# A two-layer graph network in one kernel: shared reads for the prepared sums of the second layer's weights, their low parts on GpSimd, the wait for stores taken off the sync queue, and stage 2 written out on TensorE

## The chip, the cores and the metric

One core of one Trainium2 chip. The metric is device time in microseconds of one execution. Engines: PE is TensorE, DVE is VectorE, ACT is ScalarE, POOL is GpSimd, SP is SyncE, which here does nothing but issue all DMAs of the kernel.

## The reference

```python
h = jnp.maximum(_layernorm(x, axis=-1), 0.0)          # x: 1250 x 1024
def _sage_sum(h, src, dst, Ws, Wn, b):                # Ws, Wn: 1024 x 1024
    h_neigh = jax.ops.segment_sum(h[src], dst, num_segments=N_NODES)
    return h @ Ws + h_neigh @ Wn + b
h = _sage_sum(h, src, dst, Ws1, Wn1, b1)
h = _sage_sum(h, src, dst, Ws2, Wn2, b2)
return x + h
```

There are 41,250 edges, sorted by `dst`, among 1250 nodes. All arrays are 32-bit floats.

## The kernel before, in words

The sum over neighbours is a product with a matrix A of edge counts, 1250 x 1250, so a layer is h Ws + A (h Wn) + b. Each factor is kept as a high part (rounded to the fast matmul type) and a low part (what is left), and a product is three matmuls: high by high, high by low, low by high (`PRODUCTS`). ScalarE makes a high part by a copy, another engine the low part by a subtraction.

Stage 1, to about 174 us, normalizes and transposes h into `HT`, computes y1 = h Wn1 and writes it to DRAM, and builds A in `AT`.

Stage 2 makes the first layer's output h1, transposed, in eight feature tiles of 128 columns (`feature_tile`, line 1138). A tile is two halves on TensorE. The first is 72 matmuls of `HT` with a column block of Ws1, `W_st` (lines 1146), the second 60 matmuls of `AT` with a column block of y1, `y_st` (line 1154). Both blocks have one buffer each, so block j + 1 of W_st is loaded when the first half of tile j is done (semaphore `wst_used`), and that of y_st when its second half is done (`h1_done`). ScalarE makes the high parts (lines 714, 750), VectorE the low parts (lines 966 to 974), ScalarE also writes h1 out of PSUM (`h1_save`, line 756). TensorE ran the tiles in a loop of four rounds of two.

Stage 3 computes h1 Ws2 and h1 Wn2, each by Strassen's seven products of halves: `SEQUENCE` names the 14 products, `LEFT` and `RIGHT` the blocks that are added or subtracted for each, `TARGETS` where it goes. Each product is four steps of 15 matmuls (line 1183). After it the `neighbours` products with A, and the result goes out.

In ten of the 14 products the right factor is a sum of two weight blocks, four steps each: 40 sums of 128 x 512 values. They depend on weights alone and are made during stage 2, beside the feature tiles, and parked in DRAM (`sums_dram`); stage 3 loads one at each step into `right`. A sum takes these steps, with five slots (`PREP`): SP loads both blocks into `prep_raw`, 256 KB each (line 484); GpSimd adds or subtracts them (line 635); ScalarE makes the high part (line 763); VectorE makes the low part (line 961); SP stores both parts, 512 KB (line 497).

The order of that work is written out by hand. Each engine takes its instructions strictly in the order given, and SP has all loads and stores in one such order. Per tile SP issues the load of W_st, four `prepare` steps, the load of y_st, and three `prepare` steps (`PER_TILE`, line 102), until the 40 are done in tile 6. A `prepare(i)` waits until the slot's earlier store has landed, loads the two blocks of sum i, waits for the low part of sum i - 4, and stores it. ScalarE's order in tile j is: high part of W_st j + 1, high parts of three sums, high part of y_st j + 1, h1 of tile j, high parts of four sums. When all sums are stored, SP loads the first three right factors, then b2 and a half of x, which VectorE adds together (line 984) ahead of its work for product 1.

Of the kernel before, what the change touches and what calls it, by code (L numbers as in the profile page):

```python
# [65 lines left out]
PER_TILE = (3, 4)  # L66
# [30 lines left out]
def sum_steps():  # L97

    return [n for n in range(STEPS) if right_is_sum(n // KB)]


def prepared(j, part):

    first = j * sum(PER_TILE) + part * PER_TILE[0]
    return range(first, min(first + PER_TILE[part], len(sum_steps())))

# [123 lines left out]
def gnn_kernel(nc, x, src, dst, ws1, wn1, b1, ws2, wn2, b2, out):  # L230
    edge_rows = nc.dram_tensor("edge_rows", (EROWS + P + 3, ROWX), F16, kind="Internal").ap()
    y1_dram = nc.dram_tensor("y1_dram", (N, D), F32, kind="Internal").ap()
    sums_dram = nc.dram_tensor("sums_dram", (len(sum_steps()), P, 2, HALF), F32, kind="Internal").ap()

    ctx = ExitStack()
    with ctx:
# [68 lines left out]
        prep_raw = at("prep_raw", [P, PREP, 2, HALF], F32, W0)  # L305
# [55 lines left out]
        prep_in = [sem(f"prep_in_{i}") for i in range(PREP)]; prep_stored = [sem(f"prep_stored_{i}") for i in range(PREP)]  # L361
# [33 lines left out]
        def _(sp):  # L395
# [85 lines left out]
            def quarter(n, which, to):  # L481
                what, m = SEQUENCE[n // KB]
                row, col = RIGHT[m][which]
                return sp.dma_start(to, (ws2 if what == "s" else wn2)[row * HALF + n % KB * P:row * HALF + (n % KB + 1) * P,  # L484
                                                                      col * HALF:(col + 1) * HALF])
# [12 lines left out]

            for j in range(KF):
                if j:  # L500
                    sp.wait_ge(wst_used, j)
                    load_w_st(j)
                    for i in prepared(j - 1, 1):
                        prepare(i)
# [8 lines left out]
                for i in prepared(j, 0):  # L513
                    prepare(i)
                if j == KF - 2:
                    for i in range(PREP - 1):
                        prepare(len(sum_steps()) + i)

            def load_right(n):
# [5 lines left out]
                if right_is_sum(n // KB):  # L525
                    sp.dma_start(right[:, KB - 1 - n % KB, :, :].bitcast(F32), sums_dram[right_sums(n), :, :, :]).then_inc(right_in[n % KB], 16)
                else:
                    quarter(n, 0, right_sum[:, KB - 1 - n % KB, LO, :]).then_inc(right_in[n % KB], 16)
# [6 lines left out]
            for i in range(PREP):  # L535
                sp.wait_ge(prep_stored[i], 16 * (len(sum_steps()) // PREP))
# [23 lines left out]
        def _(pool):  # L560
# [100 lines left out]
        def _(act):  # L661
# [99 lines left out]
            def prepare_high(i):  # L761
                act.wait_ge(prep_summed, i + 1)
                nc.scalar.activation(prep[:, i % PREP, HI, :], prep_raw[:, i % PREP, LO, :], ACT.Copy).then_inc(prep_hi, 1)
# [468 lines left out]
```

## Time and profile before

| | |
|---|---|
| median of 3 runs | 743.38 us (743.15 to 746.88) |
| the profiled execution's own time | 745.81 us |
| its span, first to last instruction | 744.0 us |
| TensorE, matmul busy | 663.2 us (89%) |
| VectorE, ScalarE, GpSimd busy | 307.9, 171.8, 160.8 us |
| mean granted TensorE clock | 0.949 |
| DMA | 103.1 MB, mean 139 GB/s |

Busy time is a share of the whole span and stages differ, so it says little by itself. What bounds a stage is read from the waits and from the timeline of that stage. In the rows further down L12 is line 12 of the kernel, SPq is the queue of DMA issues, PEld is TensorE's loading of weights, and "[x <-y]" behind a row is how long the engine stood idle ahead of it and what ended that. In some names the number at the end is left out.

### The profile page before, as it was taken

How to read it: one execution, taken by the hardware profiler on the slowest of the kernel's cores; microseconds unless marked ns; L12 is line 12 of the kernel's file. 1: busy time of each engine (PE TensorE's matmuls, PEld its weight loads, DVE VectorE, ACT ScalarE, POOL GpSimd, SP SyncE). 2: the span in 40 equal slices, each digit the busy share in tenths (PEclk: the TensorE clock that was granted, in tenths of full speed). 3: DMA queues.
4: the chain of work that ended last, by engine and by line, in shares of the span. 5: the costliest groups of instructions: out<-in, count | busy, mean ns of one | idle time of the engine just before them, and what ended most of it. 6: DMA issues, size and time to landing. Idle time of an engine off the chain costs nothing.

```text
span 744.0 us, 8540 instructions
## 1 busy us (share of the span) xinstructions
PE 663.2 (89%) x3280; PEld 571.7 (77%) x3280; DVE 307.9 (41%) x426; ACT 171.8 (23%) x292; POOL 160.8 (22%) x161
## 2 busy tenths in 40 slices
PE   3899999999987676786857999999999999999998
PEld 2688688878977576786757998888887778888786
DVE  3644897731322220222222225613446779731111
ACT  5443422221121210112121221221222433400000
POOL 4514340001412222222213002560311402100000
PEclk9999999999999788787879999999999999999999
DMA  8422410014456666565657456844442224111111
GB/s 297 154 49 49 123 47 32 30 56 147 171 184 220 202 210 219 171 224 182 218 188 246 143 157 216 296 150 158 154 141 73 70 84 143 56 57 57 53 57 55
DMA packets 69630, 103.10 MB, mean 139 GB/s; under 512 B 17313, under 2 KB 35755, under 8 KB 69590
## 3 DMA queue, kind: packets, MB, share of 16 engines
q1 hardware_dynamic: 69590, 102.58, 41.9%
q8 instruction: 24, 0.39, 0.2%
q14 instruction: 16, 0.13, 0.1%
HBM read 71.07 MB, written 31.48 MB: 138 GB/s over the span
## 4 chain that ended last, share of the span: by engine, by line
PE 40%; DMA 21%; issue 20%; POOL 7%; DVE 6%; SPq 4%; ACT 2%; DVEq 0%; POOLq 0%
PE PS L1058 14%; PE PS L1199 12%; DMA sums_dram<-prep 10%; PE PS L1183 6%; DMA W_st_raw<-ws_in 4%; POOL left_sum L655 4%; DMA y_st_raw<-y_dram 4%; PE PS L1050 3%; PE PS L1146 3%; SPq L484 2%; DVE prep L961 2%; POOL s L645 2%; DMA xin<-x_in 1%; DVE W_st L966 1%; DVE y_st L972 1%
## 5 line engine op out<-in xcount | busy, mean ns | idle before, releaser
L1183 PE MATMUL PS<-right,left 128*128 128x512 f32 x840 | 192.7, 390 | 2.6 <-DVE s L1002 2.1
L1183 PEld LDWEIGHTS PS<-right,left 128*128 128x128 f32 x840 | 157.0, 188 | 38.0 <-issue 5.8
L1146 PE MATMUL PS<-HT,W_st 128*128 128x416 f32 (+1 forms) x576 | 120.1, 372 | 21.8 <-DVE W_st L966 20.4
L1146 PEld LDWEIGHTS PS<-HT,W_st 128*128 128x128 f32 x576 | 115.9, 203 | 25.8 <-DVE W_st L966 22.1
L1154 PE MATMUL PS<-AT,y_st 128*128 128x416 f32 (+2 forms) x480 | 103.7, 381 | 35.9 <-DVE y_st L974 35.9
L1154 PEld LDWEIGHTS PS<-AT,y_st 128*128 128x128 f32 (+1 forms) x480 | 99.7, 209 | 39.5 <-DVE y_st L974 37.7
L1058 PE MATMUL PS<-W,HT 128*128 128x512 f32 (+1 forms) x480 | 123.3, 406 | 4.2 <-issue 2.4
L635 POOL TENSOR_TENSOR prep_raw<-prep_raw 128x512 f32<-128x512 f32 x40 | 59.7, 1494 | 239.4 <-DMA prep_raw<-ws_in 153.6
L1058 PEld LDWEIGHTS PS<-W,HT 128*128 128x128 f32 (+1 forms) x480 | 87.2, 189 | 24.4 <-issue 2.8
L655 POOL TENSOR_TENSOR left_sum<-h1T 128x640 f32<-128x640 f32 x24 | 42.5, 1773 | 173.1 <-PE PS L1183 123.7
L1199 PE MATMUL PS<-y_high,AT 128*128 128x512 f32 (+1 forms) x200 | 78.3, 392 | 0.0
L1199 PE MATMUL PS<-y_low,AT 128*128 128x512 f32 (+1 forms) x200 | 78.3, 392 | 0.0
L972 DVE TENSOR_TENSOR y_st<-y_st_raw,y_st 128x1152 fp32r<-128x1152 f32 x8 | 11.9, 1488 | 119.8 <-ACT y_st L751 119.8
L966 DVE TENSOR_TENSOR W_st<-W_st_raw,W_st 128x1024 fp32r<-128x1024 f32 x8 | 9.8, 1226 | 89.6 <-ACT W_st L714 89.6
L1199 PEld LDWEIGHTS PS<-y_low,AT 128*128 128x128 f32 (+1 forms) x200 | 37.1, 186 | 8.9
L1199 PEld LDWEIGHTS PS<-y_high,AT 128*128 128x128 f32 (+1 forms) x200 | 37.0, 185 | 8.7
L1038 DVE TENSOR_TENSOR s<-s,PS 128x512 f32<-128x512 f32 (+1 forms) x20 | 13.8, 688 | 72.1 <-PE PS L1199 72.1
L906 DVE TENSOR_TENSOR hot_n<-iota_n,pair_key 128x1600 f16<-128x1600 f16 x40 | 39.3, 983 | 0.0
L750 ACT ACTIVATE y_st<-y_st_raw 128x1152 fp32r<-128x1152 f32 x8 | 9.3, 1165 | 124.6 <-DMA y_st_raw<-y_dram 124.6
L904 DVE TENSOR_TENSOR hot_m<-iota_m,pair_m 128x1280 f16<-128x1280 f16 x40 | 33.0, 824 | 9.9 <-PE PS L1050 9.8
L1002 DVE TENSOR_TENSOR s<-s,PS 128x512 f32<-128x512 f32 (+1 forms) x60 | 36.4, 679 | 0.0
L1050 PEld LDWEIGHTS PS<-hot_n,hot_m 128*128 128x128 f16 x400 | 27.9, 97 | 8.6 <-issue 6.7
(79 smaller groups left out, 467.0 us busy)
## 6 DMA issues: line engine op xcount, KB each, us to landing
sums_dram<-prep SPq DMA_DIRECT2D x40, 512.0 KB, 4.4
right<-sums_dram SPq DMA_DIRECT2D x40, 512.0 KB, 3.4
prep_raw<-ws_in SPq DMA_DIRECT2D x40, 256.0 KB, 3.4
prep_raw<-wn_in SPq DMA_DIRECT2D x40, 256.0 KB, 3.1
y_dram<-y_out SPq DMA_DIRECT2D x18, 256.0 KB, 2.0
y_st_raw<-y_dram SPq DMA_DIRECT2D x8, 576.0 KB
s<-x_in SPq DMA_DIRECT2D x18, 256.0 KB
out<-s SPq DMA_DIRECT2D x18, 256.0 KB
```

The costliest lines, as they stand in the source:

```text
L635: nc.gpsimd.tensor_tensor(prep_raw[:, i % PREP, LO, :], prep_raw[:, i % PREP, LO, :], prep_raw[:, i % PREP, HI, :], RIGHT[SEQUENCE[n // KB ...
L655: nc.gpsimd.tensor_tensor(left_sum[:, k, LO, :], h1_block(*a, k), h1_block(*b, k), op).then_inc(left_summed, 1)
L904: nc.vector.tensor_tensor(hot_m[:, u % HOT, :, :, :], iota_m[:, :, :].unsqueeze(1).to_broadcast([P, ROW, P, 2]), pair_m[:, u, :, :].unsque ...
L906: nc.vector.tensor_tensor(hot_n[:, u % HOT, :, :, :], iota_n[:, :, :].unsqueeze(1).to_broadcast([P, ROW, NCOL, 2]), pair_key[:, u, :, :].u ...
L972: nc.vector.tensor_tensor(y_st[:, LO, 0:NT - 1, :], y_st_raw[:, LO, 0:NT - 1, :], y_st[:, HI, 0:NT - 1, :].bitcast(F32), ALU.subtract).the ...
L1002: nc.vector.tensor_tensor(c, c, PS[:r, BANKS2[g % 8], :], op).then_inc(dve_evicted, 1)
L1050: ins = nc.tensor.matmul(PS[:, COUNT_BANKS[g % 2], col:col + NCOL], hot_m[:, u % HOT, i, :, e], hot_n[:, u % HOT, i, :, e], start=i == 0, ...
L1058: ins = nc.tensor.matmul(PS[:r, bank, :], HT[:, a, k, t * P:t * P + r], W[:, k, b, :], start=first and m == 0, stop=last and m == 2)
L1146: ins = nc.tensor.matmul(PS[:, banks[c], 0:w_], W_st[:, a, k, :], HT[:, b, k, o_:o_ + w_], start=k == 0 and m == 0, stop=False)
L1154: ins = nc.tensor.matmul(PS[:, banks[c], 0:w_], y_st[:r, part, s, :].bitcast(dt), AT[:r, s, o_:o_ + w_].bitcast(dt), start=False, stop=s = ...
L1183: ins = nc.tensor.matmul(PS[:, BANKS2[g % 8], :], left[:, k, a, i * P:(i + 1) * P], right[:, KB - 1 - k, b, :], start=k == 0 and j == 0, s ...
L1199: ins = nc.tensor.matmul(PS[:rows_of(t), BANKS2[g % 8], :], AT[:r, s, t * P:t * P + rows_of(t)].bitcast(dt), y.bitcast(dt), start=s == 0 a ...
```

## The change

Four things. (1) For a chunk k of 128 rows of Ws2 or Wn2, the five sums of Strassen's scheme use only the four blocks at that chunk. These are now loaded once into a buffer `quarters`, and all five sums are made of them: eight batches of five. (2) The low parts of the sums move from VectorE to GpSimd, two sums behind. (3) SP no longer waits for a slot's store to land; GpSimd does, ahead of the sum that reuses the slot. SP waits for the low part ahead of each store, as it did. The 40 sums are spread over 14 parts, two per tile, up to tile 7. (4) TensorE's loop over the tiles is written out.

```diff
-            def prepare(i):
-
-                if i < len(sum_steps()):
-                    if i >= PREP:
-                        sp.wait_ge(prep_stored[i % PREP], 16 * (i // PREP))
-                    for which in range(2):
-                        quarter(sum_steps()[i], which, prep_raw[:, i % PREP, 1 - which, :]).then_inc(prep_in[i % PREP], 16)
-                if i >= PREP - 1:
-                    e = i - (PREP - 1)
-                    sp.wait_ge(prep_lo, e + 1)
-                    sp.dma_start(sums_dram[e, :, :, :], prep[:, e % PREP, :, :].bitcast(F32)).then_inc(prep_stored[e % PREP], 16)
+            def load_quarters(batch):
+
+                what, k = BATCHES[batch]
+                sp.wait_ge(prep_summed, batch * len(SUMS))
+                for q, (row, col) in enumerate(QUARTERS):
+                    quarter(what, row, col, k, quarters[:, q, :]).then_inc(quarter_in[q], 16)
+
+            def store_sums(part):
+                for i in prepared(part):
+                    sp.wait_ge(prep_lo, i + 1)
+                    sp.dma_start(sums_dram[i, :, :, :], prep[:, i % PREP, :, :].bitcast(F32)).then_inc(prep_stored[i % PREP], 16)
+                    batch, q = divmod(i, len(SUMS))
+                    if q == LOAD_AT and batch + 1 < len(BATCHES):
+                        load_quarters(batch + 1)
...
                     sp.wait_ge(wst_used, j)
                     load_w_st(j)
-                    for i in prepared(j - 1, 1):
-                        prepare(i)
+                    store_sums(2 * j - 1)
...
-                for i in prepared(j, 0):
-                    prepare(i)
-                if j == KF - 2:
-                    for i in range(PREP - 1):
-                        prepare(len(sum_steps()) + i)
+                if j:
+                    store_sums(2 * j)
+                else:
+                    load_quarters(0)
...
-            for i, n in enumerate(sum_steps()):
-                pool.wait_ge(prep_in[i % PREP], 32 * (i // PREP + 1))
-                nc.gpsimd.tensor_tensor(prep_raw[:, i % PREP, LO, :], prep_raw[:, i % PREP, LO, :], prep_raw[:, i % PREP, HI, :],
-                                        RIGHT[SEQUENCE[n // KB][1]][2]).then_inc(prep_summed, 1)
+            def prepare_sum(i):
+                batch, (a, b, op) = i // len(SUMS), RIGHT[SUMS[i % len(SUMS)]]
+                for block_ in (a, b):
+                    pool.wait_ge(quarter_in[QUARTERS.index(block_)], 16 * (batch + 1))
+                if i >= PREP:
+                    pool.wait_ge(prep_stored[i % PREP], 16 * (i // PREP))
+                nc.gpsimd.tensor_tensor(prep_sum[:, i % PREP, LO, :], quarters[:, QUARTERS.index(a), :],
+                                        quarters[:, QUARTERS.index(b), :], op).then_inc(prep_summed, 1)
+
+            def prepare_low(i):
+                pool.wait_ge(prep_hi, i + 1)
+                nc.gpsimd.tensor_tensor(prep[:, i % PREP, LO, :], prep_sum[:, i % PREP, LO, :], prep[:, i % PREP, HI, :].bitcast(F32),
+                                        ALU.subtract).then_inc(prep_lo, 1)
+
+            for i in range(NSUMS):
+                prepare_sum(i)
+                if i >= 2:
+                    prepare_low(i - 2)
+            for i in range(NSUMS - 2, NSUMS):
+                prepare_low(i)
...
             for j in range(KF - 1):
                 w_st_high(j + 1)
-                for i in prepared(j, 0):
-                    prepare_high(i)
+                prepare_high(2 * j + 1)
                 y_st_high(j + 1)
                 h1_save(j, j % 2)
-                for i in prepared(j, 1):
-                    prepare_high(i)
+                prepare_high(2 * j + 2)
...
-                    with pe.Fori(0, KF // 2) as q:
-                        for parity in range(2):
-                            feature_tile(q * 2 + parity, parity, dt)
+                    for j in range(KF):
+                        feature_tile(j, j % 2, dt)
```

Here `NSUMS` is 40, `LOAD_AT` is 2, and `prepared(part)` gives the sums i with 1 + 14 i // 40 equal to the part: three in most parts, two in parts 7 and 14. VectorE's `prepare_low` is gone from its order.

How SP's order moves in the tiles 2 and 3. Before, from the W_st load of tile 2 (L456; ws_in and wn_in are the weights, sums_dram the parked sums):

```order
L456 DMA W_st_raw<-ws_in 128x8x128
L484 DMA prep_raw<-wn_in 128x512 x2
L497 DMA sums_dram<-prep 128x1024
L484 DMA prep_raw<-wn_in 128x512 x2
L497 DMA sums_dram<-prep 128x1024
L484 DMA prep_raw<-ws_in 128x512 x2
L497 DMA sums_dram<-prep 128x1024
L484 DMA prep_raw<-ws_in 128x512 x2
L497 DMA sums_dram<-prep 128x1024
L509 DMA y_st_raw<-y_dram 128x9x128
```

With the change, from the same load (now L462) to the y_st load of tile 3 (L488 loads the four blocks, L501 stores a sum):

```order
L462 DMA W_st_raw<-ws_in 128x8x128
L501 DMA sums_dram<-prep 128x1024 x2
L488 DMA quarters<-ws_in 128x512 x4
L501 DMA sums_dram<-prep 128x1024
L515 DMA y_st_raw<-y_dram 128x9x128
L517 DMA y_st_raw<-y_dram 98x128
L501 DMA sums_dram<-prep 128x1024 x3
L462 DMA W_st_raw<-ws_in 128x8x128
L501 DMA sums_dram<-prep 128x1024
L488 DMA quarters<-ws_in 128x512 x4
L501 DMA sums_dram<-prep 128x1024 x2
L515 DMA y_st_raw<-y_dram 128x9x128
```

Between two loads of the tiles there stood four pairs of block loads and four stores, and now three stores and, where a batch turns, four block loads. Up to the W_st load of tile 7 these turns lie inside a part four times (as behind both L462 shown) and at a part's end three times.

The end of stage 2 on SP. Before, from the last block loads:

```order
L484 DMA prep_raw<-wn_in 128x512 x2
L497 DMA sums_dram<-prep 128x1024
L509 DMA y_st_raw<-y_dram 128x9x128
L511 DMA y_st_raw<-y_dram 98x128
L497 DMA sums_dram<-prep 128x1024 x4
L456 DMA W_st_raw<-ws_in 128x8x128
L509 DMA y_st_raw<-y_dram 128x9x128
L511 DMA y_st_raw<-y_dram 98x128
L526 DMA right<-sums_dram 128x1024 x3
L541 DMA b_sb<-b_in 128x512 x2
L532 DMA s_91<-x_in 128x512 x9
```

With the change, from the W_st load of tile 7:

```order
L462 DMA W_st_raw<-ws_in 128x8x128
L501 DMA sums_dram<-prep 128x1024 x3
L515 DMA y_st_raw<-y_dram 128x9x128
L517 DMA y_st_raw<-y_dram 98x128
L501 DMA sums_dram<-prep 128x1024 x2
L531 DMA right<-sums_dram 128x1024 x3
L547 DMA b_sb<-b_in 128x512 x2
L538 DMA s_92<-x_in 128x512 x9
```

Before, the last stores stood ahead of both loads of tile 7; now three follow its W_st load and two its y_st load, directly ahead of the loads of `right`, b2 and x.

GpSimd at the start of its sums, first before (all 40 in one row), then with the change:

```order
L635 TENSOR_TENSOR prep_raw<-prep_raw 128x512 x40
L639 MEMSET h1T 128x8x30
L655 TENSOR_TENSOR left_sum<-h1T 128x640 x8
L645 TENSOR_TENSOR s_91<-s_91,b_sb 128x512 x9
L645 TENSOR_TENSOR s_91<-s_91,b_sb 98x512
```

```order
L645 TENSOR_TENSOR prep_sum<-quarters 128x512 x3
L650 TENSOR_TENSOR prep<-prep_sum,prep 128x512
L645 TENSOR_TENSOR prep_sum<-quarters 128x512
L650 TENSOR_TENSOR prep<-prep_sum,prep 128x512
L645 TENSOR_TENSOR prep_sum<-quarters 128x512
```

The low part of sum i now stands on this engine behind sum i + 2.

## Rows read from the trace of the kernel before

**Rows 1.** The page's 40 slices of the span, TensorE's busy tenths.

```profile
PE   3899999999987676786857999999999999999998
```

**Rows 2.** Stretches of stage 2: length, busy us by engine, granted clock, DMA share, GB/s.

```profile
174.00:199.40 25.40, 25.12 (x132) 24.90 (x133) 8.92 (x6) 3.99 (x6) 8.22 (x5) 1.00 0.53 179
...
318.00:360.00 42.00, 30.35 (x133) 29.12 (x134) 10.36 (x12) 8.60 (x16) 11.00 (x8) 0.78 0.63 213
...
428.00:453.00 25.00, 25.00 (x133) 24.78 (x132) 4.59 (x6) 5.37 (x9) 0.00 (x0) 1.00 0.63 210
...
174.28:453.40 279.12, 222.82 (x1057) 215.76 (x1057) 63.38 (x67) 52.04 (x88) 59.94 (x41) 0.87 0.60 199
```

**Rows 3.** Timeline of TensorE in tile 2: start, us, and idle before.

```profile
234.45 15.48 PE L1146 MATMUL PS<-HT,W_st 128*128 128x416 f32 x72 [4.46 <-DVE W_st L966]
257.36 13.84 PE L1154 MATMUL PS<-AT,y_st 128*128 128x416 f32 x60 [7.43 <-DVE y_st L974]
```

**Rows 4.** SP's waits from 174 to 453 us: total, times, longest.

```profile
SPq L484 <- DMA sums_dram<-prep: 118.7, 35, 4.6
```

**Rows 5.** Timeline of one round of SP, ScalarE and VectorE, 226 to 268 us.

```profile
226.27 0.43 SPq L456 DMA_DIRECT2D W_st_raw<-ws_in  x1
...
232.08 1.06 ACT L714 ACTIVATE W_st<-W_st_raw 128x1024 fp32r<-128x1024 f32 x1 [14.42 <-DMA W_st_raw<-ws_in]
233.04 1.65 ACT L763 ACTIVATE prep<-prep_raw 128x512 fp32r<-128x512 f32 x3
233.17 1.23 DVE L966 TENSOR_TENSOR W_st<-W_st_raw,W_st 128x1024 fp32r<-128x1024 f32 x1 [14.01 <-ACT W_st L714]
...
247.05 0.38 SPq L509 DMA_DIRECT2D y_st_raw<-y_dram  x1
...
253.27 1.16 ACT L750 ACTIVATE y_st<-y_st_raw 128x1152 fp32r<-128x1152 f32 x1 [18.58 <-DMA y_st_raw<-y_dram]
...
254.54 1.59 ACT L756 ACTIVATE h1T<-PS,b_sb 128x416 f32<-128x416 f32 x3
...
267.04 0.43 SPq L456 DMA_DIRECT2D W_st_raw<-ws_in  x1
```

**Rows 6.** The sums' instructions, min/median/max ns, and landings; one sum beside VectorE.

```profile
L635 POOL TENSOR_TENSOR prep_raw<-prep_raw x40: 1262/1294/2489, 183.8 to 406.2; 128x512 f32<-128x512 f32 x40
...
L961 DVE TENSOR_TENSOR prep<-prep_raw,prep x40: 676/679/1785, 194.4 to 415.3; 128x512 fp32r<-128x512 f32 x40
...
DMA to landing us min/median/max: 2.6/3.3/6.3
...
L497 SPq DMA_DIRECT2D sums_dram<-prep x40: 319/430/447, 196.2 to 416.0; - x40
...
DMA to landing us min/median/max: 2.6/4.0/7.8
...
214.50 2.10 POOL L635 TENSOR_TENSOR prep_raw<-prep_raw 128x512 f32<-128x512 f32 x1 [3.36 <-DMA prep_raw<-ws_in]
```

**Rows 7.** Timeline: y_st load 0 and W_st load 1, issued to an idle queue.

```profile
177.79 0.38 SPq L509 DMA_DIRECT2D y_st_raw<-y_dram  x1
...
182.52 1.17 ACT L750 ACTIVATE y_st<-y_st_raw 128x1152 fp32r<-128x1152 f32 x1 [9.09 <-DMA y_st_raw<-y_dram]
...
188.23 0.38 SPq L456 DMA_DIRECT2D W_st_raw<-ws_in  x1
...
192.12 1.06 ACT L714 ACTIVATE W_st<-W_st_raw 128x1024 fp32r<-128x1024 f32 x1 [8.23 <-DMA W_st_raw<-ws_in]
```

**Rows 8.** Timeline of the start of stage 3, 442 to 500 us.

```profile
442.22 0.81 SPq L541 DMA_DIRECT2D b_sb<-b_in  x2
...
453.40 46.85 PE L1183 MATMUL PS<-right,left 128*128 128x512 f32 x204
...
454.12 8.86 DVE L984 TENSOR_TENSOR s<-s,b_sb 128x512 f32<-128x512 f32 x10 [14.44 <-DMA s<-x_in]
```

**Rows 9.** The page's costliest groups, the sums on GpSimd: busy, mean ns.

```profile
L635 POOL TENSOR_TENSOR prep_raw<-prep_raw 128x512 f32<-128x512 f32 x40 | 59.7, 1494 | 239.4 <-DMA prep_raw<-ws_in 153.6
```

More of the change, by code:

```diff
@@ L65 @@
 PREP = 5
-PER_TILE = (3, 4)
+QUARTERS = ((0, 0), (1, 1), (0, 1), (1, 0))
+SUMS = (1, 3, 6, 4, 7)
+BATCHES = tuple((what, k) for what in ("s", "y") for k in range(KB))
+NSUMS = len(BATCHES) * len(SUMS)
+PARTS = 2 * (KF - 1)
+LOAD_AT = 2
 def new_left(p):
@@ L94, in right_sums, with sum_of, prepared @@
     return sum(right_is_sum(q // KB) for q in range(n))
[L97 to L105, printed above, removed]
+def sum_of(n):
+    what, m = SEQUENCE[n // KB]
+    return BATCHES.index((what, n % KB)) * len(SUMS) + SUMS.index(m)
+def prepared(part):
+    return [i for i in range(NSUMS) if 1 + i * PARTS // NSUMS == part]
 def evictions():
@@ L232, in gnn_kernel @@
     y1_dram = nc.dram_tensor("y1_dram", (N, D), F32, kind="Internal").ap()
-    sums_dram = nc.dram_tensor("sums_dram", (len(sum_steps()), P, 2, HALF), F32, kind="Internal").ap()
+    sums_dram = nc.dram_tensor("sums_dram", (NSUMS, P, 2, HALF), F32, kind="Internal").ap()
     ctx = ExitStack()
@@ L359, in gnn_kernel @@
         h1_done = sem("h1_done"); h1_freed = sem("h1_freed"); h1_padded = sem("h1_padded")
-        prep_in = [sem(f"prep_in_{i}") for i in range(PREP)]; prep_stored = [sem(f"prep_stored_{i}") for i in range(PREP)]
+        quarter_in = [sem(f"quarter_in_{q}") for q in range(len(QUARTERS))]; prep_stored = [sem(f"prep_stored_{i}") for i in range(PREP)]
         prep_summed = sem("prep_summed"); prep_hi = sem("prep_hi"); prep_lo = sem("prep_lo")
@@ L478, in _, with quarter @@
                     sp.dma_start(AT[:, :, t * P:(t + 1) * P].bitcast(F32), any_cols[:, :, :]).then_inc(g_written, 16)
[L481 to L484, printed above, removed]
+            def quarter(what, row, col, k, to):
+                return sp.dma_start(to, (ws2 if what == "s" else wn2)[row * HALF + k * P:row * HALF + (k + 1) * P,
                                                                       col * HALF:(col + 1) * HALF])
[L487 to L497 removed]
+            def load_quarters(batch):
[10 more added lines that the diff above has]
+                        load_quarters(batch + 1)
             for j in range(KF):
@@ L525, in load_right @@
                 if right_is_sum(n // KB):
-                    sp.dma_start(right[:, KB - 1 - n % KB, :, :].bitcast(F32), sums_dram[right_sums(n), :, :, :]).then_inc(right_in[n % KB], 16)
+                    sp.dma_start(right[:, KB - 1 - n % KB, :, :].bitcast(F32), sums_dram[sum_of(n), :, :, :]).then_inc(right_in[n % KB], 16)
                 else:
-                    quarter(n, 0, right_sum[:, KB - 1 - n % KB, LO, :]).then_inc(right_in[n % KB], 16)
+                    what, m = SEQUENCE[n // KB]
+                    quarter(what, *RIGHT[m][0], n % KB, right_sum[:, KB - 1 - n % KB, LO, :]).then_inc(right_in[n % KB], 16)
             def load_x(half, t):
@@ L760, in _, with prepare_high @@
             y_st_high(0)
-            def prepare_high(i):
-                act.wait_ge(prep_summed, i + 1)
-                nc.scalar.activation(prep[:, i % PREP, HI, :], prep_raw[:, i % PREP, LO, :], ACT.Copy).then_inc(prep_hi, 1)
+            def prepare_high(part):
+                for i in prepared(part):
+                    act.wait_ge(prep_summed, i + 1)
+                    nc.scalar.activation(prep[:, i % PREP, HI, :], prep_sum[:, i % PREP, LO, :], ACT.Copy).then_inc(prep_hi, 1)
             for j in range(KF - 1):
                 w_st_high(j + 1)
-                for i in prepared(j, 0):
-                    prepare_high(i)
+                prepare_high(2 * j + 1)
                 y_st_high(j + 1)
                 h1_save(j, j % 2)
-                for i in prepared(j, 1):
-                    prepare_high(i)
+                prepare_high(2 * j + 2)
             def evict(p):
@@ L967, in _ @@
                                         ALU.subtract).then_inc(wst_lo, 1)
-                if j:
-                    for i in prepared(j - 1, 0):
-                        prepare_low(i)
                 dve.wait_ge(yst_hi, 2 * j + 2)
@@ L975, in _ @@
                                         y_st[:LAST, HI, NT - 1, :].bitcast(F32), ALU.subtract).then_inc(yst_lo, 1)
-                if j:
-                    for i in prepared(j - 1, 1):
-                        prepare_low(i)
             def add_bias(t):
```

11 lines of the change are left out of this document (4 added, 7 removed).

## The prediction, made before the changed kernel was run

> **What bounds the kernel now.** I read the slices of the span first [rows 1]. The reader is to see a hole: TensorE is at "9" nearly everywhere except in slices 12 to 22, where it is mostly at 6 to 8. Those slices are stage 2, the eight feature tiles. I then cut the span at the starts of the tiles [rows 2]. Tile 0 takes 25.4 us and tile 7 takes 25.0 with TensorE busy throughout at the full clock. Tile 4 takes 42.0 us with 30.4 of busy time, at a mean granted clock of 0.78; tiles 2, 3 and 5 are like it. Stage 2 as a whole lasts 279.1 us, from 174.28 to 453.40. Eight tiles at 25.4 would be 203, so some 76 us stand open.
>
> TensorE's own rows say what it waits for [rows 3]: 7.4 us ahead of tile 2's second half for the low part of y_st, and 4.5 us ahead of its first half for the low part of W_st, both made on VectorE. The waits of the queue that loads these tiles [rows 4] name the cause: within stage 2 SP stands 118.7 us, in 35 waits, for a store of `sums_dram` to land before it may load the next blocks (line 484). W_st and y_st loads are queued behind these. Stage 3 after 453.40 has no such holes.
>
> One round of that chain [rows 5] goes: W load issued at 226.27, y load at 247.05, next W load at 267.04. That is 40.8 us a round, against 25.4 of TensorE work. SP's queue, not an engine, sets stage 2.
>
> **The change, part by part.**
>
> *Loads.* Before, each of the 40 sums brings two blocks, 80 loads of 256 KB. Now 8 batches bring four blocks each: 32 loads. 48 loads of 256 KB go, 12.6 MB. At the 0.43 us that SP takes to issue a load [rows 5] that is 21 us of its time.
>
> *SP's waits.* The 35 waits for stores leave SP. They move to GpSimd, ahead of the sum that reuses the slot; a store lands after 2.6 to 7.8 us, 4.0 in the middle [rows 6], and a slot comes back five sums later, some 13 us of GpSimd time, so I cost the moved wait at nothing; if that cover is gone it is up to 7.8 us once.
>
> *What is late next.* SP still waits for `prep_lo` before every store, and its next load stands behind those stores. In a part of three sums the order is: W load, then three stores, then y load. The first store needs the first high part, and ScalarE makes that only after `w_st_high`, which waits for the very W load. So a half round is a serial chain. Low parts now alternate on GpSimd with sums two ahead, and each of these 128x512 operations is 1.29 us by its median [rows 6].
>
> W half (from the W load to the y load): landing of W, 3.9 us from an idle queue [rows 7] and 5.8 behind a pair of loads and a store [rows 5], taken as 5.0 because only a store or two are ahead of it; high part of W 0.96 (232.08 to 233.04) and of one sum 0.55 (1.65 for three) [rows 5]; first low 1.29; two more sums and lows 4 x 1.29 = 5.16; issue of the store 0.43 and hops 0.4. Sum 13.8.
>
> y half (from the y load to the next W load): landing 5.6, between 4.7 from the idle queue [rows 7] and 6.2 [rows 5]; because a store is ahead of it and its own second, small load behind; ScalarE 1.27 for y_st (253.27 to 254.54) and 1.59 for three h1 saves [rows 5]; then 0.55, 1.29, 5.16 and 0.43 as above and 0.3 for hops. Sum 16.2.
>
> *Batches.* When SP has stored the third sum of a batch it loads the next four blocks, and the fourth low part waits on GpSimd behind the first sum of those blocks. Where this falls inside a part (four times before W load 7, by the order shown) the step is 0.43 + 2 x 0.43 + 3.3 for landing (the middle value for a block, [rows 6]) + two operations 2.58 + 0.7 for hops = 7.9 in place of 2.58, so +5.3. Where it falls at the end of a part (three times) SP issues four loads, 1.7 us, and what comes behind lands about 1.6 later (a W load behind such traffic came 1.9 later, 5.8 against 3.9): +3.3.
>
> *Sum for stage 2.* W load 1 goes out at 188.2 as before [rows 7]. Six rounds follow to W load 7: 6 x (13.8 + 16.2) = 180.0; 4 x 5.3 = 21.2; 3 x 3.3 = 9.9; one part has two sums, -2.6; the first W load lands from an idle queue, -1.1. Together 207.4, so W load 7 goes out at 395.6. I leave out two small things against each other: sums run beside VectorE's low part of W (0.4 us a round), and 12.6 MB less traffic. Ready for TensorE 5.0 + 0.96 + 1.23 later, 402.8. Then a tile without waits, 25.4 [rows 2], and 1.6 for the lower clock behind the wait (tile 4, with two waits, was busy 30.4 - 25.1 = 5.3 longer; one is nearer 2): stage 3 can start at 429.8. Before it was 453.4: 23.6 us gained. The period is about 33 us a tile, so TensorE still waits.
>
> *Start of stage 3.* This part gives time back. Before, the last store was issued at 416.0 [rows 6], and x for the bias was loaded from 442.22 to 454.12, while TensorE was in tile 7 [rows 8]. Now the last stores stand behind y load 7 at 395.6 + 13.8 = 409.4: two sums, 13.2 us (16.2 less 2.6 and the issue), issued at 422.6 and landed about 3 later, 425.6. Only then do three loads of `right` go out (1.28 us), then b2 and ten loads of x. These took 11.9 us before [rows 8]; 1.5 MB of `right` ahead of them in the queue add some 3.5. x has landed at 442.3. VectorE adds the bias in 8.86 us and only then makes the first low part of the next left operand (0.8): product 1 starts at 452.0. TensorE would be there at 429.8 + 13.8 = 443.6, so it waits 8.4 us; its fourth load of `right`, behind x in the queue, is late inside the same wait. Bank 6 comes free from VectorE about 0.8 late. Before, 204 matmuls took 46.85 us from 453.40, so the 60 of a product take 13.8, and product 1 started at 467.2 with nothing late [rows 8]. Net gain: 467.2 - 452.0 - 0.8 = 14.4 us. Behind this point both versions are the same work at TensorE's pace.
>
> *Low parts off VectorE.* Before, 0.68 us each there [rows 6]; now 1.29 on GpSimd. VectorE gains 27 us of free time that nothing on the path needs. GpSimd's load goes from 40 to 80 operations, 103 us at 1.29 in some 240 us of stage 2. The Trainium skill, page "GPSIMD Engine Reference", section "8. Key points", says VectorE is "structurally ~2× faster" for elementwise work, so it speaks against this move; the rows agree, 1.29 against 0.68.
>
> *No loop on TensorE.* Costed at nothing. At loop edges of the kernel before the tile starts 0.05 us after its operand is ready (W_st low from 233.17 for 1.23, first matmul 234.45) [rows 3, 5], so the branch is hidden by the wait. Bounds: a gain of 3 x 0.05 us, and a loss of nothing, since the 204 matmuls of stage 3, which are written out already, run 46.85 us without a break [rows 8].
>
> The profiled execution took 745.8 us for a span of 744.0. By its own time: 745.8 - 14.4 = 731.4. The median of the three runs, 743.4, lies 2.4 lower, so for the median I say **729**.
>
> **The rivals.**
>
> *A, the chain is shorter than I price it.* Landings near the idle ones, 3.9 and 4.7, take 2.0 off a round, 12 us over six. For it: 12.6 MB less. Against: stores and loads still meet. About 716.
>
> *B, GpSimd becomes slower than the old waits.* Where two-input operations of both engines meet they slow down: a sum beside VectorE's y_st low took 2.10 [rows 6]. The Trainium skill has this too, on the same page and section: GpSimd shares its SBUF interfaces with VectorE, with contention for instructions with two SBUF inputs. Ten of these operations lie in each round's chain, 60 in six rounds. Gain is gone where the mean one is 14.4/60 = 0.24 longer, at 1.53 us; before, the mean of all 40 was 1.49 [rows 9]. At 2.0 us each it costs 0.71 x 60 = 43, which is 29 slower than now, about 772. Against it: in the new order VectorE has only three operations a tile, and my walk puts GpSimd's between them. A mean of 1.6 would give 748.
>
> *C, the gain is nearly eaten.* Inner batches cost 2 us more each (8) and the start of stage 3 another 3: about 740, within half a per cent.
>
> *D, the change does all it says.* SP never holds a load, tiles take 25.4, stage 3 begins at 377.5, and even with 8.4 + 0.8 given back the time is 743.4 - 75.9 + 9.2 = 677. Against it stands SP's wait for `prep_lo` ahead of each load.
>
> **How the numbers follow.** My forecast 0.50, A 0.18, C 0.14, B 0.13, D 0.05. What the measurement can tell from no change is 0.5%, 3.7 us, so the middle band is 739.7 to 747.1. Faster: forecast, A, D and the better third of C, 0.78. Same: the rest of C and B's mild end, 0.12. Slower: 0.10. The range runs from a little under A, 712, to past C, 742; D and B are left out.
>
> **What would show it.** Right: a tile period near 33 us; GpSimd's operations at 1.3 us; SP waiting on `prep_lo` and hardly at all on stores; TensorE starting stage 3 near 430, then a hole of 8 us ahead of product 1 with VectorE waiting for x. If periods are near 41, B; if near 25, D. The forecast is wrong if the sums' mean passes 1.5 us, or if product 1 starts without a hole.

## The result, and the profile after

| | before | after |
|---|---|---|
| median of 4 runs each | 743.26 us (740.40 to 746.88) | 723.03 us (719.67 to 724.28) |
| ratio after to before | | 0.972, 95% interval 0.966 to 0.977 |
| the profiled execution's own time, its span | 745.81, 744.0 us | 719.67, 717.9 us |
| VectorE, GpSimd busy | 307.9, 160.8 us | 268.0, 213.3 us |
| mean granted TensorE clock | 0.949 | 0.969 |
| DMA | 103.1 MB | 90.6 MB |

The change gains 20.2 us by the medians, and the prediction's 729 us lies 6.0 above what was measured. The profiled execution of after is its fastest and that of before lies above its median, so the two spans stand 26.1 us apart.

The slices of after, from the page; [rows 1] is their counterpart:

```profile
PE   3899999999998796799786997999999999999998
PEclk9999999999999898899989999999999999999999
```

The hole, in slices 13 to 22 here, is smaller, not gone; the 7 in slice 25 is the start of stage 3. The stretches of stage 2, of tile 1, tile 3 and tile 4, with length, busy us by engine (PE, PEld, DVE, ACT, POOL), granted clock, DMA share and GB/s, against [rows 2]:

```profile
172.81:421.54 248.73, 214.07 (x1056) 208.42 (x1057) 26.32 (x27) 52.34 (x89) 105.55 (x81) 0.92 0.48 162
197.54:226.29 28.75, 25.32 (x134) 24.40 (x133) 2.79 (x3) 6.88 (x12) 10.93 (x10) 1.00 0.50 164
259.69:297.13 37.44, 26.69 (x134) 25.68 (x133) 2.79 (x3) 6.60 (x12) 15.61 (x13) 0.89 0.52 172
297.13:326.71 29.58, 27.79 (x132) 27.04 (x133) 2.79 (x3) 6.88 (x12) 13.05 (x11) 0.90 0.49 164
```

Stage 2 takes 248.7 us in place of 279.1, 30.4 less. The third row is tile 3, the longest; it has a batch's turn inside one half and another at the end of the second. Stage 1 ended 1.5 us earlier in this execution, and stage 3 became 5.8 longer (717.9 - 421.54 = 296.4 against 290.6): 30.4 + 1.5 - 5.8 = 26.1.

What SP waits for between 174 and 460 us, against [rows 4] (total, times, longest):

```profile
SPq L501 <- POOL prep L650: 181.1, 40, 10.4
SPq L462 <- PE PS L1156: 8.0, 1, 8.0
SPq L542 <- DMA sums_dram<-prep: 2.3, 2, 1.2
```

The 118.7 us of waits for stores are gone. In their place SP waits 181.1 us, once for each of the 40 sums, for a low part on GpSimd, and in stage 2 only once for TensorE (the 2.3 us in line 542 belong to the loads of `right`). One half round in the timeline shows why, against [rows 5]:

```profile
219.07 0.43 SPq L462 DMA_DIRECT2D W_st_raw<-ws_in  x1
223.83 1.06 ACT L736 ACTIVATE W_st<-W_st_raw 128x1024 fp32r<-128x1024 f32 x1 [10.47 <-DMA W_st_raw<-ws_in]
224.79 1.65 ACT L786 ACTIVATE prep<-prep_sum 128x512 fp32r<-128x512 f32 x3
...
225.48 1.80 POOL L650 TENSOR_TENSOR prep<-prep_sum,prep 128x512 fp32r<-128x512 f32 x1 [5.54 <-ACT prep L786]
...
228.48 1.27 POOL L650 TENSOR_TENSOR prep<-prep_sum,prep 128x512 fp32r<-128x512 f32 x1
230.15 2.27 SPq L488 DMA_DIRECT2D quarters<-ws_in  x4
234.42 1.29 POOL L645 TENSOR_TENSOR prep_sum<-quarters 128x512 f32<-128x512 f32 x1 [4.67 <-DMA quarters<-ws_in]
235.67 1.29 POOL L650 TENSOR_TENSOR prep<-prep_sum,prep 128x512 fp32r<-128x512 f32 x1
236.99 0.33 SPq L501 DMA_DIRECT2D sums_dram<-prep  x1
237.43 0.38 SPq L515 DMA_DIRECT2D y_st_raw<-y_dram  x1
```

ScalarE stands idle for W_st ahead of the first high part, GpSimd stands idle 5.54 us for that high part and later 4.67 us for the batch's blocks, and the y_st load goes out only behind the last of these stores, 18.4 us after the W_st load.

### The profile page after: what moved, and what is told of

It is laid out like the page before. It is cut to its first block and busy times, and to the rows that moved or that the text cites. A ratio compares the mean times of both kernels' runs of the same rounds, so it can differ in the third digit from the quotient of the medians.

```text
span 717.9 us, 8507 instructions
## 1 busy us (share of the span) xinstructions
PE 655.6 (91%) x3280; PEld 565.7 (79%) x3280; DVE 268.0 (37%) x386; ACT 171.7 (24%) x292; POOL 213.3 (30%) x201
## 5 line engine op out<-in xcount | busy, mean ns | idle before, releaser
L1156 PE MATMUL PS<-HT,W_st 128*128 128x416 f32 (+1 forms) x576 | 118.4, 369 | 24.1 <-DVE W_st L982 23.7
L1156 PEld LDWEIGHTS PS<-HT,W_st 128*128 128x128 f32 x576 | 114.8, 201 | 27.5 <-issue 26.1
L1164 PE MATMUL PS<-AT,y_st 128*128 128x416 f32 (+2 forms) x480 | 96.8, 363 | 11.0 <-DVE y_st L987 11.0
L1164 PEld LDWEIGHTS PS<-AT,y_st 128*128 128x128 f32 (+1 forms) x480 | 93.5, 196 | 13.7 <-DVE y_st L987 12.4
L677 POOL TENSOR_TENSOR left_sum<-h1T 128x640 f32<-128x640 f32 x24 | 44.3, 1847 | 140.3 <-PE PS L1193 127.7
L645 POOL TENSOR_TENSOR prep_sum<-quarters 128x512 f32<-128x512 f32 x40 | 52.4, 1313 | 102.0 <-DMA quarters<-ws_in 82.2
L650 POOL TENSOR_TENSOR prep<-prep_sum,prep 128x512 fp32r<-128x512 f32 x40 | 55.0, 1377 | 90.1 <-ACT prep L786 90.1
L1048 DVE TENSOR_TENSOR s<-s,PS 128x512 f32<-128x512 f32 (+1 forms) x20 | 13.8, 688 | 72.0 <-PE PS L1209 72.0
L829 ACT ACTIVATE left<-left_sum 128x640 fp32r<-128x640 f32 x24 | 17.8, 740 | 70.4 <-POOL left_sum L677 70.4
```

Source lines behind the costliest of these rows:

```text
L645: nc.gpsimd.tensor_tensor(prep_sum[:, i % PREP, LO, :], quarters[:, QUARTERS.index(a), :], quarters[:, QUARTERS.index(b), :], op).then_inc ...
L650: nc.gpsimd.tensor_tensor(prep[:, i % PREP, LO, :], prep_sum[:, i % PREP, LO, :], prep[:, i % PREP, HI, :].bitcast(F32), ALU.subtract).the ...
L677: nc.gpsimd.tensor_tensor(left_sum[:, k, LO, :], h1_block(*a, k), h1_block(*b, k), op).then_inc(left_summed, 1)
L829: nc.scalar.activation(left[:, k, HI, :], whole, ACT.Copy).then_inc(left_hi, 1)
L1156: ins = nc.tensor.matmul(PS[:, banks[c], 0:w_], W_st[:, a, k, :], HT[:, b, k, o_:o_ + w_], start=k == 0 and m == 0, stop=False)
L1164: ins = nc.tensor.matmul(PS[:, banks[c], 0:w_], y_st[:r, part, s, :].bitcast(dt), AT[:r, s, o_:o_ + w_].bitcast(dt), start=False, stop=s = ...
```

## The experiments

The ratios are to the kernel before, measured beside each group of runs, with 95% intervals. Each group had its own runs of the kernel before, with medians from 743.3 to 745.0 us, so differences between medians of two groups are good to a microsecond or two. No single run makes one part of the change alone in the kernel before; the parts were taken out of the changed kernel.

| kernel | median, us | ratio |
|---|---|---|
| the change | 723.0 | 0.972 (0.966 to 0.977) |
| loop put back | 723.1 | 0.973 (0.970 to 0.975) |
| low parts on VectorE again | 682.9 | 0.921 (0.917 to 0.925) |
| SP waits for stores again | 755.2 | 1.018 (1.012 to 1.024) |
| no shared reads | 751.4 | 1.007 (1.004 to 1.011) |
| 12 parts | 730.5 | 0.979 (0.976 to 0.983) |
| high parts of sums first | 665.7 | 0.895 (0.892 to 0.899) |
| the same, low parts on VectorE, first there too | 665.9 | 0.892 (0.886 to 0.898) |
| the same, no shared reads | 677.1 | 0.906 (0.900 to 0.912) |
| SP one part behind, 12 parts | 668.4 | 0.897 (0.893 to 0.900) |
| before the change, order turned | 724.5 | 0.969 (0.963 to 0.976) |

**The loop alone.**

```diff
-                    for j in range(KF):
-                        feature_tile(j, j % 2, dt)
+                    with pe.Fori(0, KF // 2) as q:
+                        for parity in range(2):
+                            feature_tile(q * 2 + parity, parity, dt)
```

> The changed kernel with the loop of four rounds of two tiles put back on TensorE, nothing else. My theory: the branch is hidden behind waits for operands, so the time is that of the changed kernel, 723 within 1 us, and no row shows TensorE idle at the edges of tiles 1/2, 3/4 and 5/6 without a late operand. Rival: part of the 6 us that the forecast missed comes from the loop; then 725 to 730.

723.1 us, as expected. At the loop's edge between tiles 5 and 6 the timeline of TensorE shows a wait for an operand like any other:

```profile
344.66 11.60 PE L1164 MATMUL PS<-AT,y_st 128*128 128x416 f32 x60
363.01 15.75 PE L1156 MATMUL PS<-HT,W_st 128*128 128x416 f32 x72 [6.74 <-DVE W_st L982]
```

This part of the change is worth nothing here.

**Low parts back on VectorE.** On VectorE, behind the low parts of W_st and y_st as before the change:

```diff
             for i in range(NSUMS):
                 prepare_sum(i)
-                if i >= 2:
-                    prepare_low(i - 2)
...
+                if j:
+                    for i in prepared(2 * j - 1):
+                        prepare_low(i)
                 dve.wait_ge(yst_hi, 2 * j + 2)
...
+                if j:
+                    for i in prepared(2 * j):
+                        prepare_low(i)
```

> The changed kernel with the low parts of the sums made on VectorE again (behind the low part of W_st or y_st in its order), all else as changed. My theory: the low parts on GpSimd are in the chain that holds the loads of the tiles (store waits for low part, load waits for store), each sum costs the chain 2.6 us there (sum and low in turn, 1.28 each) and would cost some 0.7 on VectorE, and a batch's turn no longer holds a low part back. Walking the order with these durations, tiles take 25 to 30 us and not 27 to 37: stage 2 ends some 35 us earlier, product 1 keeps its hole of 7, and the time is 685 to 695. Rival: VectorE was relieved to good purpose (it also makes the low parts of W_st and y_st); then 723 or slower. Second rival: the landing of the loads sets the period; then no change, 720 to 726.

682.9 us: 40 us less than the change, a little more than expected. TensorE's timeline:

```profile
222.63 13.82 PE L1158 MATMUL PS<-HT,W_st 128*128 128x416 f32 x72
236.28 11.54 PE L1166 MATMUL PS<-AT,y_st 128*128 128x416 f32 x60
...
275.31 16.77 PE L1158 MATMUL PS<-HT,W_st 128*128 128x416 f32 x72 [2.45 <-DVE W_st L978]
```

Tiles take 24.7 to 25.1 us but for the fourth (27.7, with the wait at its end), the fifth (28.1, busy throughout at a granted clock of 0.89) and the seventh (26.4). So both rivals fall: relieving VectorE was to no purpose, and landings do not set the period. The move to GpSimd cost 40 us: SP's waits for low parts are 122.0 us in place of 181.1, since a low part of 0.68 us on VectorE stands in SP's chain for the 2.6 us in which GpSimd made a sum and a low part in turn.

**The waits for stores put back.**

```diff
                     sp.dma_start(sums_dram[i, :, :, :], prep[:, i % PREP, :, :].bitcast(F32)).then_inc(prep_stored[i % PREP], 16)
+                    sp.wait_ge(prep_stored[i % PREP], 16 * (i // PREP + 1))
```

> The changed kernel, but SP waits for each store to land directly after it has issued it. My theory: each such wait costs the chain the landing of a store, 2.9 us, less what GpSimd's step hides: 2.6 inside a part, nothing at its end. Twelve parts end ahead of a load of W_st or y_st up to W_st load 7: 12 x 2.9 = 35, and inside the parts about 0.6 x 24 = 14, so some 49 us more: 765 to 775, slower than before the change. Rival: the waits were hidden under GpSimd's work in the changed kernel; then 723 to 735, and what the change gained is due to fewer loads.

755.2 us: 32 more than the change and 1.8% slower than before it, but less than the 49 I had worked out. SP's waits between 172 and 450 us:

```profile
SPq L501 <- POOL prep L651: 131.2, 18, 9.9
SPq L500 <- POOL prep L651: 42.6, 21, 2.2
SPq L488 <- DMA sums_dram<-prep: 15.7, 7, 2.4
SPq L516 <- DMA sums_dram<-prep: 12.9, 6, 2.2
SPq L501 <- DMA sums_dram<-prep: 9.2, 9, 2.3
SPq L462 <- DMA sums_dram<-prep: 8.9, 4, 2.2
```

The new waits sum to 46.7 us, and those for low parts fall by 7.3 (from 181.1 to 173.8). At a part's end the wait is 2.2 and not 2.9: stores landed after 2.6 us by their median here, and the issue itself, 0.32, is part of that. The loads behind them also landed about 0.7 us sooner (W_st 3.9 by its median for 4.6 in the change, y_st 4.4 for 5.0). Both together, over twelve parts, are an estimated 17 us, what the 49 was too large by. The direction and the size against the rival (723 to 735) are settled.

**High parts of the sums first.** ScalarE's order turned, nothing else:

```diff
-                w_st_high(j + 1)
                 prepare_high(2 * j + 1)
+                w_st_high(j + 1)
+                prepare_high(2 * j + 2)
                 y_st_high(j + 1)
                 h1_save(j, j % 2)
-                prepare_high(2 * j + 2)
```

> The changed kernel with ScalarE's order turned: in each tile the high parts of the sums come ahead of the high part of W_st, and of y_st, that they stood behind. My theory: what makes the half round a serial chain is that the first high part waits for the load of W_st or y_st that SP has just issued. Turned round, SP's stores are ready when it comes to them and the loads go out at TensorE's pace: tiles of 25.4 us, stage 2 ends some 45 us earlier, the last stores lie well ahead of stage 3, product 1 starts without its hole, and the time is 670 to 680. Rival: GpSimd (80 operations, 107 us in all) or the turns of batches set the period; then tiles of 28 to 33 us, 700 to 720. Second rival: high parts of W_st and y_st now come late behind those of the sums, no gain, 720 to 730.

665.7 us, 57 less than the change, 78 less than before, and 4 below the band that I expected. The stretches of stage 2 and of one tile (columns as above):

```profile
173.53:371.76 198.23, 197.92 (x1056) 196.95 (x1057) 34.98 (x27) 54.59 (x88) 108.15 (x81) 1.00 0.62 218
222.91:247.57 24.66, 24.66 (x134) 24.60 (x134) 5.65 (x3) 6.79 (x12) 15.44 (x13) 1.00 0.59 205
```

TensorE is busy for 197.9 of 198.2 us, at the full clock. GpSimd does the same operations, and DMA moves the same 90.6 MB in less time. SP's waits show who leads now:

```profile
SPq L501 <- POOL prep L650: 74.8, 30, 6.9
...
SPq L462 <- PE PS L1156: 24.9, 6, 7.7
SPq L514 <- PE PS L1164: 20.6, 5, 6.2
```

So no engine's work bound stage 2 of the changed kernel; the order of the work did.

**No shared reads.** Each sum loads its own two blocks, issued behind the store of the sum four earlier:

```diff
-                    if q == LOAD_AT and batch + 1 < len(BATCHES):
-                        load_quarters(batch + 1)
+                    load_pair(i + 4)
...
+            def load_pair(i):
+                if i < NSUMS:
+                    (what, k), (a, b, _) = BATCHES[i // len(SUMS)], RIGHT[SUMS[i % len(SUMS)]]
...
+                    for c, (row, col) in enumerate((a, b)):
+                        quarter(what, row, col, k, quarters[:, i % 2 * 2 + c, :]).then_inc(quarter_in[i % 2 * 2 + c], 16)
```

> The changed kernel without shared reads: each sum loads its own two blocks (80 loads of 256 KB, as before the change), issued after the store of the sum four earlier, low parts on GpSimd and no wait of SP for stores as changed. My theory: SP now spends 2 x 0.43 us more per sum inside the half rounds, and 12.6 MB more traffic delays the loads of the tiles by 1 to 2 us each, against which the turns of batches (4 x 5 us) fall away: stage 2 about 10 to 20 us longer, 733 to 745. Rival: the turns of batches cost more than the extra loads; then 705 to 720 and the shared reads did harm here.

751.4 us, some 6 above the upper end expected, and 0.7% above the kernel before. Loads of W_st landed after 5.5 us by their median, against 4.6 in the change:

```profile
sums_dram<-prep SPq DMA_DIRECT2D x40, 512.0 KB, 3.0
...
W_st_raw<-ws_in SPq DMA_DIRECT2D x8, 512.0 KB, 5.5
```

With the rest as it is, taking the shared reads out costs 28 us, so the turns of batches cost less than the shared reads give. Not all of the 28 need be loads and bytes: this version has room for two pairs, so the loads for sum i + 4 follow only behind the store of sum i. Behind its first sum GpSimd waited 43 us in 23 places for blocks, where the change has 36 us in 8, and 111.2 us for high parts, where it has 90.1. No run has more room for pairs, so the shares of traffic and of room stay open.

**No shared reads, with the order turned.** The two edits above together.

> The changed kernel with ScalarE's order turned and without shared reads (two blocks per sum, 80 loads). My theory: once the chain is off the path the 48 extra loads, 21 us of issue and 12.6 MB, fit into stage 2 beside TensorE: 664 to 670, the same as with shared reads. Rival: the queue is full; then tiles of 27 to 30 us and 680 to 700.

677.1 us, 11 above the kernel that shares reads. My expectation was wrong here, and the rival came near in the time but not in its reason. SP's waits for TensorE ahead of tile loads, 45.5 us in the kernel with shared reads, are down to 2.6:

```profile
SPq L509 <- POOL prep L657: 91.2, 33, 5.8
...
SPq L520 <- PE PS L1171: 1.8, 1, 1.8
...
SPq L462 <- PE PS L1163: 0.8, 1, 0.8
```

and tiles 2 and 3 take 28.1 and 27.9 us (starts at 223.66, 251.76 and 279.65). But the queue is not full: SP stands 91.2 us waiting for low parts. Those wait for sums, and the sums for blocks that SP loads only behind a store:

```profile
336.23 1.47 SPq L488 DMA_DIRECT2D quarters<-wn_in  x2
...
342.94 1.27 POOL L652 TENSOR_TENSOR prep_sum<-quarters 128x512 f32<-128x512 f32 x1 [2.23 <-DMA quarters<-wn_in]
344.17 1.34 POOL L657 TENSOR_TENSOR prep<-prep_sum,prep 128x512 fp32r<-128x512 f32 x1
345.53 0.33 SPq L509 DMA_DIRECT2D sums_dram<-prep  x1
```

W_st lands after 6.0 us by its median, 4.1 with shared reads. So a chain holds the loads again, now through the blocks. Shared reads keep a value of 11 us when the order is right; what part of it is traffic and what part the room for only two pairs is as open as above.

**Low parts on VectorE with the order turned on both engines.** ScalarE as above, `prepare_low` on VectorE, now ahead of the low parts of W_st and y_st:

```diff
             for j in range(KF):
+                if j:
+                    for i in prepared(2 * j - 1):
+                        prepare_low(i)
                 dve.wait_ge(wst_hi, j + 1)
...
+                if j:
+                    for i in prepared(2 * j):
+                        prepare_low(i)
                 dve.wait_ge(yst_hi, 2 * j + 2)
```

> The changed kernel with ScalarE's order turned (as in the experiment with high parts first) and the low parts made on VectorE, also ahead of those of W_st and y_st. My theory: nothing is left in the way of the loads, TensorE is the bound in stage 2 either way, and where the low parts are made does not matter: 664 to 668, the same as with GpSimd. Rival: VectorE's 40 extra operations meet GpSimd's sums and delay the low parts of W_st or y_st; then TensorE's rows show waits for these and 670 to 690.

665.9 us, the same as with GpSimd. Where the low parts are made mattered only while they were in the chain.

**The kernel before the change, only the order turned.** ScalarE's and VectorE's order of the sums' parts, as in the two experiments above:

```diff
-                w_st_high(j + 1)
                 for i in prepared(j, 0):
                     prepare_high(i)
+                w_st_high(j + 1)
+                for i in prepared(j, 1):
+                    prepare_high(i)
                 y_st_high(j + 1)
                 h1_save(j, j % 2)
-                for i in prepared(j, 1):
-                    prepare_high(i)
...
+                if j:
+                    for i in prepared(j - 1, 0):
+                        prepare_low(i)
                 dve.wait_ge(wst_hi, j + 1)
...
                 if j:
-                    for i in prepared(j - 1, 0):
+                    for i in prepared(j - 1, 1):
                         prepare_low(i)
                 dve.wait_ge(yst_hi, 2 * j + 2)
```

> The kernel before the change with only the order turned: on ScalarE the high parts of the sums, and on VectorE their low parts, come ahead of those of W_st and y_st in each tile. SP still waits for stores and loads two blocks per sum. My theory: without the wait for W_st and y_st in its chain, each of SP's steps costs landing of a pair 3.3 to 3.7 plus landing of a store, some 5.1 us (235.44 to 240.68 to 245.66 in the trace of before), seven a tile, so tiles of about 36 us for tiles 2 to 5 and not 41.6: 720 to 728, about what the whole change gave. Rival: the serial order was all there was; then tiles of 25 us and 665 to 675. Second rival: no gain in this kernel, 740 to 747, and turning the order pays only where SP no longer waits for stores.

724.5 us: as much as the whole change gave. What is left are the waits of SP and late y_st loads:

```profile
265.07 13.92 PE L1146 MATMUL PS<-HT,W_st 128*128 128x416 f32 x72 [1.06 <-DVE W_st L969]
290.87 13.46 PE L1154 MATMUL PS<-AT,y_st 128*128 128x416 f32 x60 [11.88 <-DVE y_st L977]
```

```profile
SPq L484 <- DMA sums_dram<-prep: 133.1, 35, 5.9
```

The rival that the serial order was all there was falls: with stores still waited for, tiles 2 to 5 take 37 to 40 us. The change alone gives 20 us and the order alone gives 20, both together 78: with either left, the waits of SP for stores or the chain through ScalarE's order, it holds the loads.

**Twelve parts in place of 14.** `PARTS = 12`.

> The changed kernel with the 40 sums spread over 12 parts, not 14, so that the last stores are issued in tile 6 and none stands ahead of the loads of right, b2 and x. My theory: the hole of 5 us ahead of product 1 closes, but parts of three and four sums lengthen the chain in tiles 2 to 6: six more steps of 2.6 us in half rounds and the same turns of batches, against a last tile that runs free. Walked through, stage 2 ends 13 to 15 us later, the hole gives 6 to 7 back: 728 to 734. Rival: the hole is not due to the late stores; then it stays, and 735 to 740.

730.5 us, as expected. Stage 2 ended at 438.9, and the whole of product 0 and the start of product 1 run without a break:

```profile
438.92 16.82 PE L1193 MATMUL PS<-right,left 128*128 128x512 f32 x72
```

So the hole at product 1 is due to the late stores, and closing it this way costs more than it gives.

**SP one part behind.** The chain cut at another place:

```diff
-PARTS = 2 * (KF - 1)
+PARTS = 12
...
             def store_sums(part):
-                for i in prepared(part):
+                for i in prepared(part - 1):
```

> The changed kernel with SP storing in each part the sums of the part before (12 parts of sums, stores in the 13 parts from the second on), and ScalarE's order as changed, high part of W_st or y_st first. My theory: the chain can be cut at SP as well as at ScalarE. Low parts are ready when SP comes to the stores, so loads go out at TensorE's pace: tiles of 25 us, no hole, 664 to 670, like the kernel with ScalarE's order turned. Rival: what helped there was ScalarE's order in itself (high parts early), and here slots run out, since five slots hold two parts only in part; then SP waits for low parts again and tiles of 28 to 34 us, 690 to 715.

668.4 us with ScalarE's order as changed; `PARTS = 12` alone gave 730.5. Five of the tiles take 24.6 to 24.7 us. Two waits for y_st remain, 3.3 us together:

```profile
PE PS L1164 <- DVE y_st L987: 3.3, 2, 2.4
```

Two different cuts through the same chain give the same result, so it is the chain and not ScalarE's order in itself.

The best kernel here is the change with ScalarE's order turned, 665.7 us.

## Why the prediction was right, point by point

**What bounds the kernel.** Right: SP's queue set stage 2, and cutting its chain makes TensorE the bound. The prediction named the waits for stores as the cause in the kernel before; the run that only turns the order there gains 20 us, so the chain through the high parts held the loads there too.

**The waits taken off SP at nothing elsewhere.** Right. GpSimd's idle time ahead of sums is put down to the blocks' loads (97.1 us, 66.5 of it ahead of the first) and to issue (4.9), and none to a store.

**The half rounds.** Right in kind, 2 to 7% too long. From W load 7 to y load 7 it took 13.5 us (387.85 to 401.31) for 13.8 forecast; from y load 2 to W load 3 15.1 (237.43 to 252.53) for 16.2; with a batch's turn inside, 18.4 for 19.1. The terms that were mis-sized are the landings, 5.0 us and not 5.6 for y_st, 4.6 and not 5.0 for W_st, and hops. From W load 1 to W load 7, 186.53 to 387.85, passed 201.3 us for 207.4: 33.6 us a round, 1.0 less than forecast. This is half of rival A, which took 2.0 off a round: landings between the idle ones and mine. The measured 723.0 also lies midway between my 729 and its 716. Stores, too, land sooner, after 2.9 us by their median, where the page of before has 4.4.

**GpSimd's durations.** Right, and with them rival B's answer. From the views by tile, min, median and max ns, against [rows 6]:

```profile
L645 POOL TENSOR_TENSOR prep_sum<-quarters x40: 1262/1283/2414, 181.6 to 398.3; 128x512 f32<-128x512 f32 x40
...
L650 POOL TENSOR_TENSOR prep<-prep_sum,prep x40: 1260/1292/1815, 192.0 to 411.1; 128x512 fp32r<-128x512 f32 x40
```

The means are 1.31 and 1.38 us, well below the 1.53 at which the gain would be gone. The first low part of a W half runs beside VectorE's low part of W_st and takes 1.80, 0.5 more, as the 0.4 that was set against other things.

**Low parts off VectorE.** The duration was right and stood in the sum, inside the chain. What the text did not say is what the choice costs: it priced the move beside VectorE's free time and not against leaving the work there, which would have been 40 us faster. The sentence of the Trainium skill that the prediction cites ("GPSIMD Engine Reference", section "8. Key points") has VectorE about twice as fast elementwise, and the trace agrees, 0.68 us against 1.29. That is 0.6 of the 1.9 us by which a sum's step in the chain grew, from 0.68 to 2.58; the other 1.3 come from sum and low part in turn on one engine.

**The loop at nothing.** Right.

**The start of stage 3.** Right in kind, too large: 8.4 us of hole were forecast and 5.0 came. TensorE's and its neighbours' timeline, against [rows 8]:

```profile
412.47 2.65 DMA sums_dram<-prep
...
416.52 0.91 SPq L547 DMA_DIRECT2D b_sb<-b_in  x2
...
421.54 10.39 PE L1193 MATMUL PS<-right,left 128*128 128x512 f32 x45
...
432.93 6.58 DVE L994 TENSOR_TENSOR s<-s,b_sb 128x512 f32<-128x512 f32 x10 [13.82 <-DMA s<-x_in]
434.01 3.65 PE L1193 MATMUL PS<-right,left 128*128 128x512 f32 x15 [2.08 <-DMA right<-sums_dram]
...
440.31 2.37 PE L1193 MATMUL PS<-right,left 128*128 128x512 f32 x9 [2.65 <-DVE left L1029]
```

(the first row is from the chain that ended last.) Product 1 starts 18.8 us after the start of stage 3, 5.0 later than the 13.8 without a hole. The difference of 3.4 has three terms. The last store landed 6.4 us ahead of stage 3 for 4.2 forecast. VectorE added the bias in 6.6 us, not 8.9: before, two of GpSimd's left sums ran inside it (from 457.13 and 460.47, 2.1 and 2.0 us), and here one began only 1.8 us before its end; that this is the cause is likely, not tested. Against these, x landed 17.8 us behind the last store for 16.7 forecast.

**The sum.** 23.6 less 9.2 was forecast. The profile shows 30.4 less 5.8; this execution of after is 3.4 us below its median and that of before 2.6 above its own. By the medians the change gave 20.2 for 14.4 forecast. Both terms erred the same way: the gain in stage 2 was larger and the loss at stage 3 smaller. So no two errors cancelled, but the result lies as near to rival A as to the forecast.

**The parts of the change**, each undone by itself in the changed kernel: waits of SP -32, shared reads -28, low parts on GpSimd +40, loop 0. They add up to -20, what the change gave, but that is no rule: with the order turned the same parts are worth 11 us (shared reads) and 0 (low parts), so such parts need not add.

## What to carry to other kernels

When a queue issues both the loads that a fast engine waits for and the stores of side work, follow one load to the next through every engine's order: here a load waited for a store, the store for a low part, that for a high part, and that stood behind an operation on the load just issued. Cutting such a loop at one engine's order (two lines moved) gave 57 us, where the waits for stores were worth 32 and the shared reads 28. Here the side work did best ahead of the instruction that waits for a load, or a part behind on the queue; and moving it to a slower engine was free only when it was out of that loop.

## What the runs showed of the hardware that I had not expected

TensorE runs the same full tile in 25.04 or in 24.66 us (start to start), both at a granted clock of 1.00 in the profile. In the kernel with low parts on VectorE the first rows are the one (13.82 and 11.54 us), and after a wait of 2.45 us in tile 4 the later rows are the other:

```profile
303.36 13.61 PE L1158 MATMUL PS<-HT,W_st 128*128 128x416 f32 x72
316.80 11.37 PE L1166 MATMUL PS<-AT,y_st 128*128 128x416 f32 x60
```

In the turned order with low parts on GpSimd tile 2 took 24.66, with low parts on VectorE 25.04, at equal medians. Over eight tiles this is 3 us. A wait can also come with the switch the other way: in the turned order with low parts on GpSimd the last tile, after a wait of 0.31 us, has 13.89 and 11.54 where the tiles before it had 13.61 and 11.37. What switches it stays open.

VectorE's last small piece of y_st's low part (98x128) took 1.36 to 1.38 us in six of eight tiles before the change, each time beside a sum on GpSimd, and 0.28 or 0.29 in the other two, where none ran. In the change it took 0.28 or 0.29 in seven of eight, where GpSimd is idle at that moment:

```profile
211.62 0.29 DVE L987 TENSOR_TENSOR y_st<-y_st_raw,y_st 98x128 fp32r<-98x128 f32 x1
```

The small operation thus pays 1.1 us, nearly a whole sum on the other engine (1.29 alone), and the sum beside it took 2.1 to 2.5 us in five tiles.
